# TensorE's values and due steps between the two score products, in the three attentions with heads of 16

## What is computed

```python
# L0: self-attention with a causal mask, and cross-attention on the same x
att = where(causal, q @ k.T * scale, -inf);  y  = softmax(att) @ v
attc = qc @ kc.T * scale;                    y += softmax(attc) @ vc
x = x + y @ Wp + bp
# L1 and L3: one attention over the context, keys and values from ctx (no mask)
x = x + (softmax(q @ k.T * scale) @ v) @ Wo + bo
```

## Time and profile before

| | |
|---|---|
| median of 3 runs | 3547.6 us (3528.22 to 3549.84) |
| span of the profiled execution | 3554.1 us |
| instructions | 44786 |
| busy: TensorE, VectorE, ScalarE, GpSimd | 2891.2, 1989.7, 1455.8, 1138.3 us |
| mean granted TensorE clock | 0.871 of full |

### The profile page before, as it was taken

The page is one execution under the profiler, slowest core; times in us unless marked ns, Lnnn a source line. Parts: engine busy times, 40 slices in busy tenths (PEclk is TensorE's granted clock), DMA queues, the critical chain, the costliest instruction groups (busy, mean ns, idle before and its releaser), DMA issues. The chain is left out here.

```text
span 3554.1 us, 44786 instructions
## 1 busy us (share of the span) xinstructions
PE 2891.2 (81%) x16756; PEld 1619.2 (46%) x16756; DVE 1989.7 (56%) x3631; ACT 1455.8 (41%) x1932; POOL 1138.3 (32%) x1007
## 2 busy tenths in 40 slices
PE   5988898758877879999876889878999998688544
PEld 2333333533324544444662334357778777233222
DVE  4545545756654735444574666655454443566588
ACT  1354455415552224444422545432433432356422
POOL 2122222221222225555513767741010010222233
PEclk7698889878887999999986989979999999689766
DMA  6354454034531001111100000000221221464100
GB/s 161 71 110 100 101 114 108 19 70 91 105 77 42 1 18 35 40 41 62 61 7 12 1 1 1 13 12 16 76 77 46 67 63 48 99 113 96 30 15 15
DMA packets 129735, 198.50 MB, mean 56 GB/s; under 512 B 36272, under 2 KB 66480, under 8 KB 129392
## 3 DMA queue, kind: packets, MB, share of 16 engines
q1 hardware_dynamic: 97776, 143.23, 17.7%
q0 software_dynamic: 31744, 52.41, 5.4%
HBM read 130.73 MB, written 64.75 MB: 55 GB/s over the span
## 5 line engine op out<-in xcount | busy, mean ns | idle before, releaser
L2248 DVE TENSOR_REDUCE L_mx<-bank_t 128x2 f32<-128x1024 f32 (+3 forms) x512 | 562.7, 1122 | 485.8 <-PE bank_t L2056 312.5
L2248 DVE TENSOR_REDUCE L2a_mx<-bank_t 128x2 f32<-128x1024 f32 x256 | 311.3, 1223 | 392.3 <-PE bank_t L2033 391.6
L2455 ACT ACTIVATE L_P<-bank_t 128x1024 f32<-128x1024 f32 (+3 forms) x384 | 348.6, 919 | 372.5 <-PE bank_t L2070 198.1
L2455 ACT ACTIVATE L2a_P<-bank_t 128x1024 f32<-128x1024 f32 x256 | 261.9, 1024 | 289.7 <-PE bank_t L2045 289.3
L2070 PE MATMUL bank_t<-L_QS,L_KS 50*128 50x512 f32 (+2 forms) x1024 | 244.1, 480 | 114.1 <-DVE L_mx L2248 86.5
L2056 PE MATMUL bank_t<-L_KS,L_QS 48*128 48x512 f32 (+2 forms) x1024 | 264.1, 518 | 76.9 <-DMA L_QS<-L_spill_q_halves 64.8
L2033 PE MATMUL bank_t<-L2a_QK 32*128 32x512 f32 x1536 | 251.9, 445 | 71.9 <-DVE L2a_mx L2248 28.1
L2041 PE MATMUL bank_t<-L2a_QK 32*128 32x512 f32 x1536 | 258.5, 446 | 0.0
L2056 PEld LDWEIGHTS bank_t<-L_KS,L_QS 48*128 48x128 f32 x1024 | 108.8, 211 | 325.1 <-issue 223.2
L2033 PEld LDWEIGHTS bank_t<-L2a_QK 32*128 32x128 f32 x1536 | 136.7, 196 | 235.9 <-ACT L2a_P L2455 109.7
L2570 POOL TENSOR_TENSOR L_lo<-L_full,L_hi 128x512 fp32r<-128x512 f32 x64 | 81.2, 1268 | 423.0 <-ACT L_hi L2442 409.3
(11 more groups left out here) (431 smaller groups left out, 6224.3 us busy)
## 6 DMA issues: line engine op xcount, KB each, us to landing
L_KS<-L_spill_k_halves SPq DMA_DIRECT2D x174, 128.0 KB, 4.6
L_QS<-L_spill_q_halves SPq DMA_DIRECT2D x174, 128.0 KB, 5.0
L_spill_raw<-xn POOLq DMA_DIRECT2D x64, 256.0 KB, 2.4
L2g_raw<-in_L_ffn_h_blocks SPq DMA_DIRECT2D x32, 512.0 KB, 3.7
L_spill_k_halves<-L_hi SPq DMA_DIRECT2D x32, 256.0 KB, 2.1
L_spill_k_halves<-L_lo SPq DMA_DIRECT2D x32, 256.0 KB, 2.3
L_spill_q_halves<-L_hi SPq DMA_DIRECT2D x32, 256.0 KB, 4.7
L_spill_q_halves<-L_lo SPq DMA_DIRECT2D x32, 256.0 KB, 5.0
```

Source lines behind the costliest of these rows:

```text
L2248: e.tensor_reduce(neg, s.tile[:, :, 0:n_keys], AX.X, ALU.max, negate=True).then_inc(sem(s.done), 1)
L2455: e.activation(s.at.Pr[s.pb][:, :, q0:S], s.tile[:, :, q0:S], ACT.Exp, scale=s.at.scale).then_inc(sem(s.exp), 1)
```

## The change

In the attentions with heads of 16, the due work of a tick (the values, the chore and all follow-ups) is added to the list after the scores for the maximum and before the logits. Before, it was added after the logits. For heads of 32 it stays behind both; there only the adding of partial sums (`add_up`) changes its place in the list of delayed steps against other steps of the same tick.

```diff
-            def probabilities(un, s, kt, fed):
+            def probabilities(un, s, kt, fed, between):
...
                     else:
                         add(Scores(step, None))
                     add(step)
+                if D == 16:
+                    between()
                 if not together:
                     add(Scores(None, logits))
                 add(logits)
                 tiles.free[i_t] = [e_p]
+                if D == 32:
+                    between()
                 return pb, e_p, i_d, e_m
...
                             fed = feed(at_tick + lead + 1)
-                            parts.append(probabilities(un, g * at.GP + p, kt, fed))
+
+                            def other_work(p=p):
+                                if len(pending) > lag:
+                                    pending.pop(0)()
+                                if at_tick == prep_at:
+                                    queue_up(new)
+                                run_due(chore=any_tick or p == at.GP - 1 or (pooled and len(chores) > 2))
+                            parts.append(probabilities(un, g * at.GP + p, kt, fed, other_work))
                             if pooled:
-                                later(1, lambda un=un, p=p, place=place, part=parts[-1]: add_up(un, p, place, part))
-                            if len(pending) > lag:
-                                pending.pop(0)()
-                            if at_tick == prep_at:
-                                queue_up(new)
-                            run_due(chore=any_tick or p == at.GP - 1 or (pooled and len(chores) > 2))
+                                delayed.append((tick[0], lambda un=un, p=p, place=place, part=parts[-1]: add_up(
+                                    un, p, place, part)))
                             at_tick += 1
```

## The result

The changed kernel takes 3479.4 us (median of 4 runs, 3474.6 to 3483.7) against 3548.7 for the kernel before on the same chip. The ratio is 0.9835, with a 95% interval of 0.9808 to 0.9863: 1.65% or 58 us less. The forecast was 3509, with a range of 3462 to 3556. The direction was right and the size somewhat too small.

What follows compares the result with a forecast made beforehand. The prediction took TensorE, stalled in three loops by logits waiting for VectorE's maximum, as the bound. Its terms, 24 + 16 - 17 + 8 + 2 - 4 + 10 = 39 us, took 3547.6 to 3509 us, range 3462 to 3556.

Steps and rivals of the forecast that it cites:

- What bounds the kernel: In the L0, L1 and L3 loops, TensorE's logits wait for VectorE's maximum: 86.5 us in 120 cases, below 25 afterwards.
- The exchange of owner: In two ticks of the loops, the wait passes from VectorE to ScalarE; period 3.26 to 2.96 us, 0.30 gained.
- The sum of idle time: In the three loops, the terms without the clock: 24 + 16 - 17 + 8 + 2 - 4 = 29 us.
- The whole in three parts: The predicted gain by kind: 29 us of idle time in the loops, 10 from the clock, nothing outside the loops.
- What stands behind ScalarE's moved copies: On ScalarE, copies ahead of their tick's exponential make it late: 17 us lost; projections waiting for `L_hi` give 8 back.
- the given-back part: Over the loops, projections and turned maxima wait less for the bank `L_hi` frees: 8 us of about 15.
- The copy of the values and the reciprocal behind it: On ScalarE, 20 bare copies delay exponentials 0.3 us each; the earlier copy and VectorE's reciprocal gain 2 us.
- What swallows some of it: In L0 and L3, a unit's first scores wait for query halves through DRAM: 4 us lost, between 0 and 10.
- The clock: In the loops TensorE's lower clock level held 297 us; shorter waits gain 10 us, between 0 and 46.
- the rival in which the clock follows: In the loops, shortened waits keep TensorE's clock from falling: 36 us more gained, 3473 us; chance 0.17.
- GpSimd's sums in L2: In L2, a few GpSimd sums change places with neighbours of their own tick; costed at nothing.
- ScalarE as the bound: Exponentials behind copies in every unit hold up TensorE: 58 us instead of 17, 3550, or 3568 without clock gain; chance 0.10.

Runs made afterwards that it cites:

- the second profile: The changed kernel itself measured once more, beside other kernels on the same chip and in more rounds: 3489.3 us, ratio 0.9852 to before.
- L2's sums only: Kernel before with nothing but the new place of `add_up` in L2's attention: 3532.2 us, ratio 0.9995.
- all copies behind: Changed kernel with TensorE's new order, but ScalarE takes each exponential ahead of its tick's copies, as before (except ticks with a next-stage step): 3551.8 us, ratio 1.0048.
- half the maximum: Heads of 16 reduce only half the keys, which changes the computation: in kernel before 3483.6 us, 0.9838; in the changed kernel 3456.7 us, 0.9761.
- the stack's copies behind: Changed kernel, but only the two copies of a projected stack stand behind their tick's exponential on ScalarE: 3526.0 us, ratio 0.9966.
- the mixed kernel: Changed kernel in L0; in L1 and L3 only chore and follow-ups stand between the score products, values behind the logits: 3472.9 us, ratio 0.9814.
- due work only: Changed kernel, but only chore and follow-ups stand between the two score products, the values behind the logits as before: 3509.3 us, ratio 0.9916.
- values in halves: Changed kernel with the values' 8 matmuls issued as two sets of 4, one in each tick of a pair: 3519.9 us, ratio 0.9947.

## Why the prediction was right, and where it was not

- **What bounds the kernel** (the logits' waits for the maximum, with work that could fill them right behind): right. They fell from 86.5 to 14.9 us; below 25 was said.
- **The exchange of owner:** right. The new wait of scores for an exponential is 45.1 us in 83 cases at 0.54 each (20 to 40 us at about 0.4 were said, so it came out larger), and the period is 3.05 us (2.96). The 0.09 us between them lie mostly in the step from logits to exponential, 0.54 where the earlier trace rows had given 0.44.
- **The sum of idle time:** right in size. Without the clock the terms are 24 + 16 - 17 + 8 + 2 - 4 = 29 us; TensorE's idle time in the loops fell by 22 (26 by the second profile). Of the loops, L0 and L3 fell by 36 and 16 us and L1 by 7, the clock included.
- **The whole in three parts:** on the mean of two profiles each (before and L2's sums only; the change twice) the loops lost 24 us of idle time and 24 of busy time, and the rest of the span 9. The prediction had 29, 10 and nothing.
- **"What stands behind ScalarE's moved copies":** this step failed. It costed the new place of the copies at 17 us lost and 8 given back, so that TensorE's new order alone would have been 9 us better than the change. Alone it is slower than before (1.0048) and has 30 us more idle time than the changed kernel. I had priced the given-back part from the waits for `L_hi` in kernel before. In the loops these are 10.9 us with the turned maxima (not 15), and they fell to 7.7; `L_hi` ahead of projections was to be halved and went from 0.61 to 0.37 us each. But this was the wrong place to look. In kernel before, the values lie between a V tick's logits and the next projection, and give the copies time. Moved ahead of those logits they no longer do, and the same copies in their old place are waited for: in L1 and L3 1.8 us for each such projection with only the values moved, and 2.04 with the projection moved as well, instead of 0.6; over the span, turned maxima included, 36.6 and 44.8 us instead of 19.3. The copies' move prevents a cost that TensorE's move brings; it isn't an extra with a price of its own. What I costed as a loss behind them, late exponentials, is small: the waits for exponentials are 38.9 us with all copies behind and 43.6 to 45.1 with them in front, so 5 or 6 us instead of 17.
- **The copy of the values and the reciprocal behind it:** 20 x 0.3 us of cost and 2 us of gain; the kernel with this copy behind is within its interval of the change. Right to be small.
- **"What swallows some of it":** the mechanism is real (half the maximum in kernel before), but in the change the waits for query halves went from 64.8 to 60.7 us over the span, and those for the rows of the maximum from 21.5 to 15.5. 4 us were taken for it; none shows.
- **"The clock":** right in kind, mis-sized. 10 us were taken, up to 46 allowed. Of the 58 us 22 to 26 are idle time in the loops, which leaves 32 to 36. TensorE's busy time in the loops, with the same matmuls, fell by 24 of them on the mean of two profiles each (893.1 and 874.8 for before and L2's sums only, 857.4 and 862.2 for the change), with the clock at 0.87 and 0.89, then 0.91 and 0.90 (0.86 to 0.90 was said). The other 10 or so lie outside the loops, where the order is as before but for L2's sums. There the two profiles of the order before have 2508.6 and 2507.4 us, those of the change 2494.0 and 2503.6; as these last two differ by 10 with nothing changed, it isn't shown that this part belongs to the change., on which the 10 us rested, had in its slow stretch three waits of 0.47 to 0.70 us, not up to 0.9. The result lies between the forecast and the rival in which the clock follows (3473). The Trainium skill, "TensorE: Matmul & The Clock Gate", section "A second HAM failure mode: psum-queue depth-cycling", says that short idle stretches between groups of matmuls on rotating banks make the clock swing; the traces here agree in part: three of six projections ran at near half speed right after 2.04 us of waiting, the other three did not, and all six ran at full speed after 0.37; and where TensorE's idle time in the loops was only 11 us, its clock was 0.98.
- **GpSimd's sums in L2** at nothing: right (0.9995).
- **ScalarE as the bound:** did not come; the scores' waits for exponentials stayed below the 60 us that would have marked it.

What stays open: why half the maximum speeds up the changed kernel by 26 us or more with hardly less idle time, which other copies make up the 0.8% between the stack's copies behind and all copies behind, how much of the time outside the loops belongs to the change, and whether the mixed kernel beats the change.

## What to carry to other kernels

When work on one engine is moved ahead of a wait to cover it, look at what it covered in its old place: here the values moved forward had given another engine time to copy out the bank that the next projection needs, and only with these copies moved in the same step did the change pay in full. Test two such moves as a square of four kernels, since alone one was worth +0.5%, the other -0.4%, and both together -1.65%. And compare a loop's idle time between profiles, not its length, where the clock of the engine that bounds it moves between runs.

## What the runs showed of the hardware

- **Between the two ends of the table a microsecond of waits was worth about two.** From the slowest order to the fastest the idle time in the loops falls by 45 us (160.1 to 115.1), the time by 2.3% or 83 us. The busy time of the same matmuls in the loops falls by 41 us (888.3 to 847.4), at a granted clock of 0.88 and 0.92. From one kernel to the next it doesn't hold: due work only has the change's idle time and half of its gain. With the same order, one profile of before and that of L2's sums only differ by 18 us in the loops at equal idle time.
- **Small matmuls side by side.** The values' matmuls write 32 columns each, four heads to four column groups. Eight of them, over all four groups, take 0.99 us; four of them, over two groups, take 0.99 us too, so a set that leaves half of the groups empty costs as much as a full one. One by one, four of the eight start within 0.02 us and the other four 0.45 us later; of the half set two start together, and the other two 0.45 us later. The Trainium skill, "TensorE: Matmul & The Clock Gate", section "Part 3: Packing small matmuls — row/col tiling", says that matmuls at different tile positions run at the same time; these starts agree. A split by queries, which would keep all four groups filled, wasn't tried.
- **Being busy isn't being fast.** With the values in halves TensorE's clock was 0.98 to 0.99 and its idle time 11 us in the loops, and they took 1025.0 us, against 987.4 at 130 us of idle time.
